# Expert ranks of the first batch moved into the last slot and tail of the first attention of a four-stage kernel

## The chip, the cores and the metric

One core of a Trainium2 chip runs the whole program. The metric is the device time of one execution in microseconds (us); lower is better. Before the change three runs gave 1869.03 (median), 1868.91 and 1872.07 us.

The engines are named as the profile names them: PE (TensorE; PEld is its weight loads), DVE (VectorE), ACT (ScalarE), POOL (GpSimd) and SP (the queue that issues the transfers).

## What is computed

Four residual stages run over 4 batches of 256 tokens of width 512, all in float32. Cut to what matters:

```python
x = x + attention0(layernorm(x))   # 32 query heads, 8 key heads, causal softmax
x = x + experts(layernorm(x))      # 64 experts of rank 16, top 16 of each token
x = x + attention1(layernorm(x))   # RMS norms of q and k, slopes on the distance
x = x + ffn(layernorm(x))          # 4-bit codes times block maxima, silu(g) * u

def experts(x):
    scores = x @ Wr.T
    gates = softmax(top_k(scores, 16))
    h = einsum('nd,krd->nkr', x, A)          # the "ranks"
    return einsum('nkr,kdr->nd', h * G[:, :, None], B) * SCALING
```

## The kernel before

Each float32 product is made of three PE instructions on a high and a low half of each operand (`mm3`, lines 312 to 314). So every operand is first split: a copy to `..._hi` on ACT or POOL, and a subtraction to `..._lo` on DVE or POOL.

Each attention runs over 8 groups of 4 heads, with one key head to a group. Inside a group there is one **slot** for each batch. A slot computes masked scores and softmax of its batch, multiplies the slot before's probabilities with the values (`pv`), adds the slot before's output to `x` (`out` 0 and 1), and makes three weight tiles (K, Q0, Q1 or Q2, Q3, V) of the coming group. The order inside a slot is a hand-written list of steps, one list for all engines: every engine walks the same list and takes from it what is its own (`slot_steps`, `first_slot_steps`, `last_slot_steps`, `tail_steps`, `lead_steps`). An engine does its instructions strictly in that order, and waits on counters (semaphores) of the others. Seven turns of a loop make the slots 1, 2, 3 and 0; a first slot stands ahead, and the last slots 1, 2, 3 and a tail behind it.

Results of PE go through two banks of a ring (`pe_ring_bank`): a tile may start once the tile two places before was read by DVE. So the tile Q1 waits for `kt_lo`, the low half of the tile K.

The first attention also decodes a part of the last stage's weights beside its own work: in each slot POOL centres the codes (`code_early`, line 537), ACT makes eight lines of them in two halves of four (`dq_lines` 0 and 1, line 546), DVE takes their maxima (`dq_top`), and POOL multiplies (`dq_value`). In the second attention POOL splits the next weights (`w_next`, lines 570 and 571) and the normed keys (`k_norm` on POOL, line 1019 and then 570 and 571), for whose end the next slot's scores wait (line 705).

Between two stages the layer norm of each batch runs: `norm_stats` on DVE, `norm_root` on POOL (some 16 short steps, one after the other), `norm_write` on ACT (`xn`, line 473), and `norm_turn`, in which PE transposes `xn` (line 460) and ACT and DVE split the result into `xt_hi` and `xt_lo` (lines 483 and 490). In the last slots batch 0 is normed in slot 2, batch 1 in slot 3, batch 2 in the tail, and batch 3 in the next stage.

The experts' stage (`expert_steps`) splits the router's matrix and the matrix A in pieces (`split_a` 0 to 4: ACT to `a_hi`, DVE to `a_lo`, lines 1328 and 1402), POOL writes the pattern `spread`, then PE makes the router's scores and the ranks of each batch in 4 units of 24 matmuls. DVE's `router` makes the gates from the scores, ACT and DVE split them (`turn_gates`), and PE spreads them (`gated`, lines 1300 and 1302). The two transfers of A and the router's matrix are issued by SP at 653 us of the trace, during the last slot 1.

Semaphores keep memory apart: `a_hi`, `a_lo` and `ranks` lie where the first attention's queries and keys lay.

## Time and profile before

| what | us |
|---|---|
| median of three runs | 1869.03 |
| lowest and highest run | 1868.91, 1872.07 |
| the profiled execution, its own time | 1863.55 |
| its span in the trace | 1861.8 |
| PE busy | 1751.9 (94%) |
| DVE busy | 1296.9 (70%) |
| ACT busy | 877.7 (47%) |
| POOL busy | 788.6 (42%) |

The trace is of one execution. Its span leaves out 1.75 us around it. Busy time of PE counts matmuls, whose ends are modelled. A wait in the trace is idle time of an engine ahead of one instruction, put down to the instruction that ended it.

### The profile page before, as it was taken

To read this page: it belongs to the slowest core of one execution; us is meant where nothing else is said; L and a number is where in the kernel's file an instruction comes from. 1 tells how busy PE (TensorE), PEld (TensorE's weight loads), DVE (VectorE), ACT (ScalarE), POOL (GpSimd) and SP (SyncE) were. 2 spreads that over 40 slices of the span, in tenths; PEclk is the share of its full clock that TensorE was granted. 3 is DMA by queue.
4 is the path that set the end of the run, shared out by engine and by line. 5 is a ranking of instruction groups with operands and counts; after the bars stand their busy time and mean duration, and the time that the engine had idled before them with its cause. 6 is when DMAs were issued, how large, how long until landed. Compare 5 with 4: busy or idle time off the path is not lost.

```text
span 1861.8 us, 28756 instructions
## 1 busy us (share of the span) xinstructions
PE 1751.9 (94%) x8864; PEld 1449.6 (78%) x8864; DVE 1296.9 (70%) x2317; ACT 877.7 (47%) x2288; POOL 788.6 (42%) x924
## 2 busy tenths in 40 slices
PE   8999999999999977997899999999999997889999
PEld 7787878788787866885778787878787886668887
DVE  5787778777788765345677777877777776655555
ACT  3556565556555634222444444444444444454543
POOL 5334425262534433144545454545454424244442
PEclk9999999999999998999899999999999999999999
DMA  4022122121112121000101000000001002022121
GB/s 143 33 68 73 60 64 90 43 95 65 62 62 77 47 71 57 1 7 23 35 29 28 28 29 28 28 28 28 28 28 28 23 0 80 0 69 68 56 56 46
DMA packets 47711, 87.77 MB, mean 47 GB/s; under 512 B 6576, under 2 KB 6576, under 8 KB 47536
## 3 DMA queue, kind: packets, MB, share of 16 engines
q1 hardware_dynamic: 47664, 87.19, 14.8%
q8 instruction: 24, 0.39, 0.1%
q14 instruction: 23, 0.19, 0.0%
HBM read 77.73 MB, written 9.44 MB: 47 GB/s over the span
## 4 chain that ended last, share of the span: by engine, by line
PE 54%; DVE 6%; POOL 4%; ACT 3%; issue 2%; POOLq 0%; DVEq 0%; ACTq 0%
PE ring L312 10%; PE ring L314 9%; PE ring L313 9%; PE scores L312 3%; PE scores L314 3%; PE scores L313 3%; PE turned L312 3%; PE turned L313 3%; PE turned L314 3%; PE scores L705 2%; PE turned L791 1%; PE turned L755 1%; PE turned L756 1%; PE turned L777 1%; PE turned L784 1%
## 5 line engine op out<-in xcount | busy, mean ns | idle before, releaser
L312 PE MATMUL ring<-xt_hi,w_lo 128*128 128x512 f32 x768 | 306.3, 399 | 18.9 <-DVE kt_lo L930 14.9
L313 PE MATMUL ring<-xt_lo,w_hi 128*128 128x512 f32 x768 | 304.7, 397 | 0.0
L314 PE MATMUL ring<-xt_hi,w_hi 128*128 128x512 f32 x768 | 304.5, 397 | 0.0
L312 PE MATMUL ring<-wd_hi,ot_lo 128*128 128x512 f32 x512 | 208.3, 407 | 8.2 <-DVE ot_lo L906 6.4
L804 ACT CAST pt_hi<-turned 128x512 fp32r<-128x512 f32 x192 | 100.6, 590 | 237.7 <-PE turned L784 231.0
L313 PE MATMUL ring<-wd_lo,ot_hi 128*128 128x512 f32 x512 | 203.7, 398 | 0.0
L314 PE MATMUL ring<-wd_hi,ot_hi 128*128 128x512 f32 x512 | 203.6, 398 | 0.0
L312 PEld LDWEIGHTS ring<-xt_hi,w_lo 128*128 128x128 f32 x768 | 145.6, 190 | 53.9 <-issue 19.1
L570 POOL TENSOR_SCALAR sq_hi<-sq 128x512 fp32r<-128x512 f32 x80 | 55.0, 687 | 305.4 <-ACT sq L830 286.9
L314 PEld LDWEIGHTS ring<-xt_hi,w_hi 128*128 128x128 f32 x768 | 145.3, 189 | 34.9
L546 ACT ACTIVATE lv_early<-code_early 128x512 f32<-128x512 f32 x224 | 122.6, 631 | 102.9 <-POOL code_early L537 95.0
L313 PEld LDWEIGHTS ring<-xt_lo,w_hi 128*128 128x128 f32 x768 | 145.7, 190 | 31.4
L900 DVE TENSOR_TENSOR p<-p,rsum 128x512 f32<-128x512 f32 (+1 forms) x128 | 150.1, 1173 | 4.4
L862 DVE TENSOR_TENSOR pt_lo<-turned,pt_hi 128x512 fp32r<-128x512 f32 x192 | 120.8, 683 | 35.9 <-ACT pt_hi L804 35.9
L830 ACT ACTIVATE sq<-ring 128x512 f32<-128x512 f32 x80 | 48.3, 604 | 191.6 <-PE ring L314 183.5
L813 ACT ACTIVATE p<-scores,bias,root 128x128 f32<-128x128 f32 (+1 forms) x256 | 128.0, 519 | 19.0 <-DVE bias L890 19.0
L561 POOL TENSOR_TENSOR deq_early<-lv_early 128x512 f32<-128x512 f32 x28 | 37.9, 1354 | 228.8 <-DVE lv_early L555 196.9
L571 POOL TENSOR_TENSOR w_lo<-w_raw,w_hi 128x512 fp32r<-128x512 f32 x96 | 130.2, 1356 | 8.0
L930 DVE TENSOR_TENSOR qt_lo<-ring,qt_hi 128x512 fp32r<-128x512 f32 x128 | 88.1, 688 | 61.7 <-ACT qt_hi L840 60.3
L911 DVE TENSOR_TENSOR x<-x,ring 128x512 f32<-128x512 f32 x128 | 87.0, 682 | 53.4 <-PE ring L314 52.8
L570 POOL TENSOR_SCALAR w_hi<-w_raw 128x512 fp32r<-128x512 f32 x96 | 77.0, 802 | 110.9 <-DMA w_raw<-w_attn_dram 57.4
L906 DVE TENSOR_TENSOR ot_lo<-turned,ot_hi 128x512 fp32r<-128x512 f32 x128 | 83.5, 685 | 57.7 <-ACT ot_hi L819 57.6
(247 smaller groups left out, 4480.6 us busy)
## 6 DMA issues: line engine op xcount, KB each, us to landing
w_raw<-w_attn_dram SPq DMA_DIRECT2D x96, 256.0 KB, 3.1
wd_raw<-w_dense_dram SPq DMA_DIRECT2D x64, 256.0 KB, 2.7
code_early<-codes_dram SPq DMA_DIRECT2D x28, 256.0 KB, 2.8
absmax_early<-absmax_dram SPq DMA_DIRECT2D x56, 128.0 KB, 3.0
kept_dram<-deq_early SPq DMA_DIRECT2D x28, 256.0 KB, 2.0
stage<-kept_dram SPq DMA_DIRECT2D x28, 256.0 KB, 2.7
code_late<-codes_dram SPq DMA_DIRECT2D x14, 256.0 KB, 2.7
absmax_late<-absmax_dram SPq DMA_DIRECT2D x28, 128.0 KB, 2.9
```

What stands on the lines that cost most here:

```text
L312: nc.tensor.matmul(o, l_lo, r_hi, start=start, stop=False)
L313: nc.tensor.matmul(o, l_hi, r_lo, start=False, stop=False)
L314: return nc.tensor.matmul(o, l_hi, r_hi, start=False, stop=stop)
L546: ins = nc.scalar.activation(lv[:, q, :], code[:, par, :], ACT.Copy, bias=offset, scale=scale)
L570: pool_link(nc.gpsimd.tensor_scalar(dst_hi, src, 1.0, 0.0, ALU.mult, ALU.add))
L571: nc.gpsimd.tensor_tensor(dst_lo, src, as_f32(dst_hi), ALU.subtract).then_inc(sem_done, 1)
L804: nc.scalar.copy(pt_hi[:, j, :, :], turned[:, j, :, :]).then_inc(s_pt_hi, 1)
L813: ins = nc.scalar.activation(pr[:, h, :], sc[:, h, :], ACT.Exp, bias=bias[:, k, h:h + 1], scale=scale, accum_out=sums[:, k, h:h + 1])
L862: nc.vector.tensor_tensor(pt_lo[:, j, :, :], turned[:, j, :, :], as_f32(pt_hi[:, j, :, :]), ALU.subtract).then_inc(s_pt_lo, 1)
L900: nc.vector.tensor_tensor(pr[:, :, :], pr[:, :, :], rsum[:, k, :].unsqueeze(2).to_broadcast([P, HEADS, width]), ALU.mult).then_inc(s_prob, 1)
L911: dve_ring_free(nc.vector.tensor_tensor(x[:, t, :], x[:, t, :], tile, ALU.add))
L930: dve_ring_free(nc.vector.tensor_tensor(lo, tile, as_f32(hi), ALU.subtract))
```

## The change

It rewrites the lists of steps; of computing instructions none is added or taken away. The parts:

1. **Slot 2 of the first attention**: the first half of the code lines (`dq_lines` 0) stands behind `pv` on ACT, as in slot 1 already, and no longer ahead of the tile K.
2. **First slots**: in the first attention the second softmax part (`exp` 1) and its normalising stand ahead of the tiles Q0 and Q1; in the second one `normalise` 1 stands ahead of `q_rms` and `v_turn`.
3. **Slot 3 of the second attention**: POOL splits the normed keys ahead of the two next weight tiles.
4. **Last slots of both**: `norm_write` of a batch stands one slot later, behind the probabilities' split, and `norm_turn` behind `pv`. In slot 1 of the second, `k_norm` stands behind the code splits and `out` 1.
5. **First attention into the experts**: `split_a` 0 to 2 in the last slot 3, `split_a` 3 and 4, `spread` and the first two units of batch 0's ranks in the tail. They now wait for the last scores of the attention rather than for its last ring tile. `norm_turn` 2 and the other two units stand in the experts' stage, ahead of and behind the router's step, and `norm_turn` 3 behind the first `gated`.
6. **Second attention into the last stage**: `norm_turn` 2 stands behind the first `unit` (24 matmuls).
7. `b_hi` and `b_lo` lie behind the experts' small buffers.

```diff
-    s = [("pt_split",)] + ([] if rms or b == 1 else [("dq_lines", 0)])
+    s = [("pt_split",)] + ([] if rms or b in (1, 2) else [("dq_lines", 0)])
...
-    s += [("pv",)] + ([("exp", 1)] if rms else [("dq_lines", 0)] if b == 1 else [])
+    s += [("pv",)] + ([("exp", 1)] if rms else [("dq_lines", 0)] if b in (1, 2) else [])
...
+    s += [("k_norm", 1 if b == 1 else 0)] if roots else []
     s += [("w_next", X) for X in (Q0, Q1)] if rms and b == 3 else []
-    s += [("k_norm", 1 if b == 1 else 0)] if roots else []
...
-        s += [("w_next", Q0)] + softmax[2] + [("tile", V, 1, 0), ("q_rms", 1, 1), ("w_next", Q1), ("v_turn", 1)]
-        return s + [("normalise", 1)] + [("w_next", X) for X in (Q2, Q3, V)] + [("transpose",)]
-    s = softmax[0] + [("tile", K, 1, 0)] + softmax[1] + [("tile", Q0, 1, 0)] + softmax[2] + [("tile", Q1, 1, 0)]
-    return s + [("normalise", 1), ("dq_first",), ("transpose",)]
+        s += [("w_next", Q0)] + softmax[2] + [("tile", V, 1, 0), ("normalise", 1), ("q_rms", 1, 1), ("w_next", Q1)]
+        return s + [("v_turn", 1)] + [("w_next", X) for X in (Q2, Q3, V)] + [("transpose",)]
+    s = softmax[0] + softmax[1][0:1] + [("tile", K, 1, 0)] + softmax[1][1:] + softmax[2] + [("tile", Q0, 1, 0)]
+    return s + [("normalise", 1), ("tile", Q1, 1, 0), ("dq_first",), ("transpose",)]
...
-    s = [("pt_split",)] + ([("norm_turn", 0)] if b == 3 else []) + ([("scores", 0)] if b == 1 else [])
+    s = [("pt_split",)] + ([("norm_write", 0, "act")] if b == 3 else []) + ([("scores", 0)] if b == 1 else [])
...
-        s += [("mask", 0), ("pv",)]
+        s += [("mask", 0), ("pv",)] + ([("norm_turn", 0)] if b == 3 else [])
...
-    s += [("normalise", 0), ("exp", 1), ("normalise", 1), ("out", 0)]
-    s += [("k_norm", 1)] if rms and b == 1 else []
+    splits = [("expert", ("split_a", p)) for p in range(3)] if b == 3 and not rms else []
+    s += [("normalise", 0), ("exp", 1), ("normalise", 1)] + splits[0:2] + [("out", 0)] + splits[2:3]
...
-    s += [("norm_write", b - 2, "act")] if b >= 2 else []
-    s += [("out", 1)] + ([("scores", 1)] if b < 3 else [])
+    s += [("out", 1)] + ([("k_norm", 1)] if rms and b == 1 else []) + ([("scores", 1)] if b < 3 else [])
...
-def tail_steps():
-
-    return [("pt_split",), ("norm_turn", 1), ("pv",)] + norm_begin([2], "pool") + [("norm_write", 2, "act"), ("out", 0), ("out", 1),
-                                                                 ("norm_turn", 2)]
+def tail_steps(rms):
+
+    if rms:
+        s = [("pt_split",), ("norm_write", 1, "act"), ("pv",), ("norm_turn", 1)] + norm_begin([2], "pool")
+        return s + [("out", 0), ("out", 1), ("norm_write", 2, "act")]
+    s = [("pt_split",), ("expert", ("split_a", 3)), ("norm_write", 1, "act"), ("expert", ("spread",))]
+    s += [("expert", ("ranks", 0, 0)), ("pv",), ("norm_turn", 1), ("expert", ("split_a", 4))]
+    s += norm_begin([2], "pool") + [("expert", ("ranks", 0, 1)), ("out", 0), ("out", 1), ("norm_write", 2, "act")]
+    return s
...
-            s = [("split_a", 0)] + head(0) + [("split_a", p) for p in range(1, UNITS + 1)] + [("router", 0)]
-            s += norm_begin([3], "pool") + ranks(0)[0:2] + [("norm_write", 3, "act")] + ranks(0)[2:4]
-            s += [("norm_turn", 3)]
-            s += gated(0) + [("router", 1)] + [("split_b", p) for p in range(UNITS)] + ranks(1) + [("out", 0)]
+            s = [("scores", 0)] + ranks(0)[2:3] + [("turn_scores", 0), ("norm_turn", 2), ("router", 0)]
+            s += norm_begin([3], "pool") + ranks(0)[3:4] + [("norm_write", 3, "act")]
+            s += gated(0) + [("norm_turn", 3), ("router", 1)] + [("split_b", p) for p in range(UNITS)] + ranks(1) + [("out", 0)]
...
-                            eng.wait_ge(s_ring_free, attention_tiles[0])
+                            eng.wait_ge(s_scores, GROUPS * BATCH)
...
-            opening += norm_begin([3], "dve") + [("silu", 0), ("h", 0), ("h_hi", 0), ("norm_turn", 3), ("h_lo", 0)]
+            opening += [("norm_stats", [3]), ("norm_root", [3], "dve"), ("norm_turn", 2), ("norm_write", 3, "dve")]
+            opening += [("silu", 0), ("h", 0), ("h_hi", 0), ("norm_turn", 3), ("h_lo", 0)]
```

How the built instructions move, at three places. **ACT, slot 2 of the first attention's loop.** `lv_early` are the code lines, `kt`, `qt` the tiles K and Q0 (then Q1), `p` the softmax, `ot` the product `pv`. Before:

```order
L804 CAST pt_hi<-turned 128x512
L543 REGISTER_ALU
L546 ACTIVATE lv_early<-code_early 128x512 x4
L368 REGISTER_ALU
L835 COPY kt_f<-ring 128x256
L836 CAST kt_hi<-ring 128x512
```

With the change:

```order
L813 CAST pt_hi<-turned 128x512
L372 REGISTER_ALU
L844 COPY kt_f<-ring 128x256
L845 CAST kt_hi<-ring 128x512
...
L822 ACTIVATE p,sums<-scores,bias 128x256 x4
L828 CAST ot_hi<-turned 128x512 x2
L550 ACTIVATE lv_early<-code_early 128x512 x4
L372 REGISTER_ALU
L848 COPY qt_f<-ring 128x256
L849 CAST qt_hi<-ring 128x512
```

The four lines moved from ahead of the tile K to ahead of the copies of the tile Q1.

**ACT, from the first attention's tail to the experts' first gates.** Before:

```order
L819 CAST ot_hi<-turned 128x512 x2
L473 ACTIVATE xn<-x,shift,rstd 128x512 x2
L483 CAST xt_hi<-ring 128x4x128 x2
L1328 CAST a_hi<-a_raw 128x4x64
L1328 CAST a_hi<-a_raw 128x4x256 x4
L1336 ACTIVATE gate<-score,top_neg 128x64 x2
L1346 COPY ranks<-scores 128x512 x2
L473 ACTIVATE xn<-x,shift,rstd 128x512 x2
L1346 COPY ranks<-scores 128x512 x2
L483 CAST xt_hi<-ring 128x4x128 x2
L1352 CAST gates_hi<-scores 64x256
```

With the change:

```order
L1339 CAST a_hi<-a_raw 128x4x256
L1357 COPY ranks<-scores 128x512
L477 ACTIVATE xn<-x,shift,rstd 128x512 x2
L1357 COPY ranks<-scores 128x512
L487 CAST xt_hi<-ring 128x4x128 x2
L1347 ACTIVATE gate<-score,top_neg 128x64 x2
L1357 COPY ranks<-scores 128x512
L477 ACTIVATE xn<-x,shift,rstd 128x512 x2
L1363 CAST gates_hi<-scores 64x256
```

The splits of A and two of the four copies of ranks went ahead; the last `xn` here is batch 3's, and `gates_hi` still stands right behind it, with one unit of ranks ahead of it in place of four.

**POOL, slot 3 of the second attention's loop.** Before:

```order
L570 TENSOR_SCALAR w_hi<-w_raw 128x512
L340 REGISTER_ALU
L571 TENSOR_TENSOR w_lo<-w_raw,w_hi 128x512
L1017 REGISTER_ALU
L1019 TENSOR_SCALAR kt_f<-k_raw 128x256
L570 TENSOR_SCALAR kt_hi<-k_raw 128x512
```

With the change:

```order
L1032 TENSOR_SCALAR kt_f<-k_raw 128x256
L574 TENSOR_SCALAR kt_hi<-k_raw 128x512
L344 REGISTER_ALU
L575 TENSOR_TENSOR kt_lo<-k_raw,kt_hi 128x512
L574 TENSOR_SCALAR w_hi<-w_raw 128x512
```

The keys' three instructions moved ahead of the four of the next weights Q0 and Q1.

## Rows read from the trace of the kernel before

**Rows 1.** The profile's page, its first part: busy us, share, instructions.
```profile
PE 1751.9 (94%) x8864; PEld 1449.6 (78%) x8864; DVE 1296.9 (70%) x2317; ACT 877.7 (47%) x2288; POOL 788.6 (42%) x924
```

**Rows 2.** Busy PE, PEld, DVE, ACT, POOL, then clock: first attention's end.
```profile
660.00:741.00 81.00, 61.69 (x331) 51.41 (x330) 46.65 (x96) 33.20 (x77) 23.86 (x109) 0.85 0.11 42
```

**Rows 3.** PE's waits over the whole trace: total us, times, longest.
```profile
PE ring L312 <- DVE kt_lo L930: 14.9, 6, 2.7
PE ring L460 <- ACT xn L473: 14.9, 7, 3.5
PE scores L705 <- POOL kt_lo L571: 10.7, 7, 1.7
...
PE turned L777 <- DVE q_slope L960: 4.1, 1, 4.1
```

**Rows 4.** Timeline, PE, starts of slots 2 and 3, first and second loop turn.
```profile
75.44 0.39 PE L705 MATMUL scores<-kt_f,qt_f 128*128 128x128 f32 x2
...
95.16 0.39 PE L705 MATMUL scores<-kt_f,qt_f 128*128 128x128 f32 x2
...
155.03 0.39 PE L705 MATMUL scores<-kt_f,qt_f 128*128 128x128 f32 x2
...
179.17 0.39 PE L705 MATMUL scores<-kt_f,qt_f 128*128 128x128 f32 x2
```

**Rows 5.** Timeline, ACT and PE in slot 2 of the second turn.
```profile
163.90 0.63 ACT L546 ACTIVATE lv_early<-code_early 128x512 f32<-128x512 f32 x1 [7.97 <-POOL code_early L537]
...
167.68 0.49 PE L312 MATMUL ring<-xt_hi,w_lo 128*128 128x512 f32 x1 [2.52 <-DVE kt_lo L930]
```

**Rows 6.** Timeline, PE, starts of slots 3 and 0, second attention, first and seventh turn.
```profile
950.94 0.28 PE L705 MATMUL scores<-kt_f,qt_f 128*128 128x128 f32 x1
...
975.56 0.38 PE L705 MATMUL scores<-kt_f,qt_f 128*128 128x128 f32 x1 [1.70 <-POOL kt_lo L571]
...
1493.77 0.39 PE L705 MATMUL scores<-kt_f,qt_f 128*128 128x128 f32 x2
...
1516.50 0.28 PE L705 MATMUL scores<-kt_f,qt_f 128*128 128x128 f32 x1
```

**Rows 7.** Timeline, PE, the waits ahead of the second transposes of both first slots.
```profile
51.56 1.97 PE L791 MATMUL turned<-ident,p 128*128 128x128 f32 x8 [2.86 <-DVE p L900]
...
904.69 1.97 PE L791 MATMUL turned<-ident,p 128*128 128x128 f32 x8 [2.49 <-DVE p L900]
```

**Rows 8.** PE's waits from 660 to 741 us, the first three.
```profile
PE ring L460 <- ACT xn L473: 9.0, 4, 3.5
PE turned L312 <- DVE pt_lo L862: 4.5, 3, 1.7
PE ring L312 <- DVE xt_lo L490: 3.6, 2, 2.3
```

**Rows 9.** Busy time by stretch, the stretches at half clock between 660 and 741.
```profile
679.00:686.00 7.00, 5.78 (x14) 4.59 (x15) 5.17 (x9) 2.37 (x5) 0.00 (x0) 0.52 0.00 0
696.00:702.00 6.00, 4.77 (x15) 3.82 (x16) 3.60 (x6) 3.73 (x8) 0.00 (x0) 0.50 0.00 0
713.00:723.00 10.00, 6.70 (x30) 6.14 (x31) 6.59 (x9) 4.58 (x6) 4.83 (x7) 0.50 0.00 1
```

**Rows 10.** Groups by line and shape, 700 to 760 us: busy us, mean ns.
```profile
L1402 DVE TENSOR_TENSOR a_lo<-a_raw,a_hi 128x1024 fp32r<-128x1024 f32 x4 | 4.6, 1218 | 0.0
```

**Rows 11.** Timeline, DVE and ACT, batch 3's norm and the first gates.
```profile
726.56 1.28 DVE L399 BATCH_NORM_STATS2 bn<-x 128x6 f32<-128x512 f32 x2
...
732.59 1.52 ACT L473 ACTIVATE xn<-x,shift,rstd 128x512 f32<-128x512 f32 x2 [4.81 <-POOL shift L448]
...
735.91 0.38 ACT L1352 CAST gates_hi<-scores 64x256 fp32r<-64x256 f32 x1
...
736.79 0.40 DVE L1410 TENSOR_TENSOR gates_lo<-scores,gates_hi 64x256 fp32r<-64x256 f32 x1
```

**Rows 12.** PE's waits from 1540 to 1620 us, the first.
```profile
PE ring L460 <- ACT xn L473: 5.9, 3, 2.7
```

More of the change, by code:

```diff
@@ L1175, in expert_steps @@
         def expert_steps():
-            head = lambda b: [("scores", b), ("turn_scores", b)]
             ranks = lambda b: [("ranks", b, u) for u in range(UNITS)]
@@ L1243, in sp, with pe_steps @@
                 eng.dma_start(b_raw, lora_b).then_inc(s_lora_raw[1], 16)
-            def pe(eng):
-                scores_at = 0
-                for step in expert_steps():
-                    b = step[1]
+            scores_at, out_at = [0], [0]
+            def pe_steps(eng, steps):
+                for step in steps:
+                    b = step[1] if len(step) > 1 else None
                     if step[0] == "scores":
@@ L1317, in pe, with act_steps @@
                         pe_norm_turn(eng, b)
-            def act(eng):
-                out_at = 0
-                for step in expert_steps():
-                    b = step[1]
+            def act_steps(eng, steps):
+                for step in steps:
+                    b = step[1] if len(step) > 1 else None
                     if step[0] in ("split_a", "split_b"):
@@ L1365, in act, with pool_steps @@
                         act_ring.take()
[L1366 removed]
+                        out_at[0] = act_ring.n
                     elif step[0] in NORM_STEPS:
                         act_norm(eng, step)
[L1370 to L1381 removed]
+            def pool_steps(eng, steps):
+                for step in steps:
+                    if step[0] == "spread":
+                        eng.wait_ge(s_scores, GROUPS * BATCH)
+                        ones = ranks[0:EXPERTS, EC // 2:EC, :].rearrange("p c d -> p (c d)")
+                        pool_link(nc.gpsimd.memset(ones, 1.0))
+                        pool_link(nc.gpsimd.affine_select(out=ones, in_=ones, compare_op=ALU.is_ge, fill=0.0, base=0,
+                                                          pattern=[[1, ER]], channel_multiplier=-RANK))
+                        pool_link(nc.gpsimd.affine_select(out=ones, in_=ones, compare_op=ALU.is_ge, fill=0.0,
+                                                          base=RANK - 1, pattern=[[-1, ER]], channel_multiplier=RANK))
+                        nc.gpsimd.tensor_scalar(spread[:, :], ones, 1.0, 0.0, ALU.mult, ALU.add).then_inc(s_spread, 1)
+                    elif step[0] == "gated":
                         eng.wait_ge(s_gated_hi, UNITS * step[1] + step[2] + 1)
@@ L1394, in pool, with dve_steps @@
                         pool_norm(eng, step)
-            def dve(eng):
-                for step in expert_steps():
-                    b = step[1]
+            def dve_steps(eng, steps):
+                for step in steps:
+                    b = step[1] if len(step) > 1 else None
                     if step[0] in ("split_a", "split_b"):
@@ L1454, in router, with pe, act, dve @@
                                         ALU.mult).then_inc(s_gates, 1)
+            behind_first["pe"], behind_first["act"] = pe_steps, act_steps
+            behind_first["dve"], behind_first["pool"] = dve_steps, pool_steps
+            def pe(eng):
+                pe_steps(eng, expert_steps())
+            def act(eng):
+                act_steps(eng, expert_steps())
+            def dve(eng):
+                dve_steps(eng, expert_steps())
+            def pool(eng):
+                pool_steps(eng, expert_steps())
             return pe, act, dve, pool, sp
```

41 lines of the change are left out of this document (19 added, 22 removed).

## The prediction, made before the changed kernel ran

> **What bounds the kernel now.** I read the page's first part first: PE is busy for 1751.9 of 1861.8 us [rows 1]. So PE is the bound, and what a change of order can win is the 110 us in which PE stands, and stretches in which its clock is halved. The other engines have room on the whole (DVE 70%), so the question is only where they are late for PE. PE's waits over the whole trace answer that [rows 3]: `kt_lo` on DVE 14.9 us in 6 waits, `xn` on ACT 14.9 in 7, `kt_lo` on POOL 10.7 in 7. The first and the third repeat 6 or 7 times, which says "loop", the second belongs to the ends of the attentions. The end of the first attention is the worst place: PE is busy for 61.7 of 81 us at a mean clock of 0.85 [rows 2]. The change touches all of these places. I go through it by place.
>
> **Loop of the first attention, slot 2 (part 1).** The starts of the scores give the length of a slot. Slot 2 takes 95.16 − 75.44 = 19.72 in the first turn, and 179.17 − 155.03 = 24.14 in the second [rows 4]; the later ones are alike (their mean is 24.10). Slots 1, 3 and 0, which have the same matmuls, also take about 20. What is lost is seen on ACT [rows 5]: it sits idle for 7.97 until POOL has centred the codes (`code_early`), then makes four lines (0.63 the first, 2.2 together), and only then copies the tile K. So `kt_lo` comes late, and PE waits 2.52 ahead of Q1's matmuls; six such waits make the 14.9 [rows 3]. The rest of the 4.4 is a wait for `ot_lo` or PE at half clock behind the wait. With the change ACT goes to the tile K at once. The gain is at most 6 × (24.10 − 19.72) = 26.3.
>
> Some is given back. The four lines, 2.2, now stand behind `pv` and ahead of the copies of tile Q1. So `qt_hi` comes up to 2.2 later, with it `qt_lo` and the next normalising on DVE, and the maxima that POOL's next centring waits for. By my count PE feels 0.8 of it in each slot 2, in all 7 turns: 5.6. Slot 1 has this very order and takes 20, which excludes more than about 2 in a slot while the centre is on time. Term: −26.3 + 5.6 = **−20.7**; bounds −26.3 (nothing given back) and −11 (the whole 2.2 in each turn).
>
> **Loop of the second attention, slot 3 (part 3).** The slot takes 975.56 − 950.94 = 24.62 in the first turn, and 1516.50 − 1493.77 = 22.73 in the seventh [rows 6]. In the seventh there are no next weights to split, so POOL's queue is free: that measures the slot without the queue. The first ends in a wait of 1.70 for POOL's `kt_lo`, one of seven [rows 3]. With the keys ahead of four POOL instructions the wait is gone, and the weights are needed a slot later, so nobody waits for them instead. Term: 6 × (24.62 − 22.73) = **−11.4**; bounds −11.4 and −8 (the six waits of 1.70 less some loss elsewhere).
>
> **First slots (part 2).** PE waits 2.86 and 2.49 for the normalised `p` [rows 7]. In the second attention the normalising jumps two items of DVE and the wait goes whole; in the first only an exponential and one tile's subtraction are passed, of which I expect 1.6. Term: −1.6 − 2.5 = **−4.1**; bounds −5.3 and −1.5.
>
> **From the first attention's last slots to the experts (parts 4, 5).** This is one stretch, from the last transposes of slot 2 to the first ranks of batch 1. PE's work in it at full clock stays. Its three largest sorts of wait are `xn` 9.0, `pt_lo` 4.5, `xt_lo` 3.6: together 17.1 [rows 8]. And the clock is at 0.50 in three stretches, in which PE is busy for 5.78 + 4.77 + 6.70 us; half of that, 8.6, is lost [rows 9]. With the change `xn` is written a slot ahead of its transposes and ranks stand in the gaps, so these waits go. New ones come:
>
> - the tail's `pv` waits for `pt_lo`, behind which DVE now has pieces of A, at 1.218 each [rows 10]: 1.5;
> - in slot 3 two short ones, for `pt_lo` 1.7 and for the ring's `xt_lo` 0.9, and two of 0.75 together;
> - the first gates' transposes wait for DVE's router, since only two units of ranks are left to stand over it: 1.9;
> - the first `gated` waits for `gates_lo`. Before, 736.79 + 0.40 − 726.56 = 10.6 us passed from the start of batch 3's statistics to the end of `gates_lo`; without the copies in between it is 6.0 to the start of `xn`, 2 × 0.76 for `xn`, 0.38 and 0.40 for the two halves of the gates: 8.4 [rows 11]. Four units of ranks lay over it; now PE has only 1.9 us of work there (the gates' transposes and batch 1's scores). Wait: 8.4 − 1.9 = 6.5.
>
> New waits: 1.5 + 3.35 + 1.9 + 6.5 = 13.3, so waits win 17.1 − 13.3 = 3.8. Clock: the stretches at half clock lie behind pauses of PE. The first two have no such pause any more; behind the one of 6.5 I expect one like the last, 6.70 / 2 = 3.4. That wins 8.6 − 3.4 = 5.2. Term: **−9.0**; bounds −14 (the gates are met in time, no half clock) and −3 (half clock stays as it is and the short waits double).
>
> The rule of the Trainium skill, "TensorE: Matmul & The Clock Gate", section "What's actually happening", speaks against this: "the default state is throttled, and activity releases the throttle", so a new gap charges more than its length. The trace agrees as far as it goes, with 0.50 behind the present gaps.
>
> **End of the second attention (parts 4, 6).** The three waits for `xn`, 5.9 us [rows 12], go in the same way, and so do those that follow from them; some 0.6 comes for `pt_lo`: −5.3. Against it stands the last slot 1: its `k_norm` now follows two code splits on POOL and `out` 1, while the next scores wait for the keys. Before, PE waited 4.1 there for `q_slope` [rows 3]; I expect 5.5, so +1.4. Term **−3.9**; bounds −6 and +1.
>
> Part 7 moves memory alone; SP's queue has the same transfers in the same order, and A is loaded at 653, ahead of its first new split. I cost both at nothing.
>
> **Sum.** −20.7 − 11.4 − 4.1 − 9.0 − 3.9 = −49.1. The profiled execution took 1863.55, so 1814.5; the median of the runs lies 5.5 above that execution, so 1820.0. All bounds low: 26.3 + 11.4 + 5.3 + 14 + 6 = 63.0, 1806. All high: 11 + 8 + 1.5 + 3 − 1 = 22.5, 1846.5.
>
> **Rivals.**
>
> *A, the lines pile up.* ACT now has both halves of the code lines behind `pv`, close together. If the chain of centring, lines and maxima then runs late in each turn, the gain of slot 2 comes back as later waits for `ot_lo` and `p`: 26.3 − 7 × 2.7 leaves 7 us in place of 20.7, 1834. For it speaks that the lines waited for POOL by 7.97 [rows 5]; against it slot 1.
>
> *B, the boundary gives nothing.* The gap of 6.5 at the first gates plus PE at half clock for as long as in the last stretch, and one more such stretch at the tail: the term is between 0 and −4, and the time 1825 to 1829. For it speaks that the gates' half is still queued behind batch 3's `xn` on ACT.
>
> *C, slower.* The decoding of the early weights is one chain per tile (POOL centres, ACT makes two halves, DVE takes two maxima, POOL multiplies). By my count a tile takes 20.1 us, as long as a slot, and the wait at slot 2 was its slack. If moving the lines back makes this chain the bound, each of the 28 slots is longer. It decides from (26.3 + 28.3) / 28 = 1.95 us a slot, the 28.3 being the other terms (11.4 + 4.1 + 9.0 + 3.9, rounded); at 2.5 a slot the result is 70 − 54.7 = +15.3, 1884. Against it: slots 1, 3 and 0 take the same 20 us with the chain running beside them.
>
> *D, nothing is given back.* The copies of Q1 have slack: 1814.
>
> **How the numbers follow.** Forecast 0.60, A 0.15, B 0.15, D 0.07, C 0.03. The range reaches over D's neighbourhood and A: 1808 to 1837, leaving out C and the outer ends of the bounds. A measurement of this kernel tells 0.2%, 3.7 us, from no change. All cases but C are faster by far more; of their 0.97 I keep 0.01 for a mixture that comes out even: 0.96, 0.01 and, for C, 0.03.
>
> **What the changed profile would show.** Right: slot 2 of the first attention takes some 20.5 in all seven turns and `kt_lo` on DVE is gone from PE's waits; slot 3 of the second takes 22.7 in all; batch 1's ranks start near 732; one wait of 6 to 7 for `gates_lo` ahead of the first `gated`. A shows as waits of 2 to 3 for `ot_lo` or `p` in slots 2 and 3; B as a clock of 0.5 from 720 on; C as slots of 22 us throughout. If slot 2 still takes 24, or if the lines are found to wait for POOL again and hold back `qt_hi`, the largest term is wrong.

## The result, and the profile after

The changed kernel takes 1813.65 us (median of 4 runs, 1807.24 to 1818.03); the kernel before, run beside it, 1868.97. The ratio is 0.9699, with a 95% interval from 0.9666 to 0.9732: 3.0% faster. Predicted were 1820.0 and a range of 1808 to 1837. The profiled execution took 1811.87 (span 1810.2), where the sum made for it said 1814.5.

The page's first part, beside [rows 1]:

```profile
PE 1736.5 (96%) x8864; PEld 1443.1 (80%) x8864; DVE 1295.3 (72%) x2317; ACT 877.6 (48%) x2288; POOL 787.8 (44%) x924
```

PE has the same instructions and is busy 15.4 us less, so a part of the gain is clock. The granted clock is given as a share of full speed: 1.00 is full, 0.50 half, and a value between them is the mean of a stretch that has both. Over the whole trace it rose from 0.981 to 0.986. An estimate from these two means: (1 − 0.981) × 1861.8 = 35.4 us of full speed were withheld before and (1 − 0.986) × 1810.2 = 25.3 now, 10 less, a part of it in PE's pauses. PE's waits over the whole trace (total us, times, longest), beside [rows 3]:

```profile
PE turned L316 <- DVE pt_lo L873: 9.8, 6, 1.9
PE scores L712 <- POOL kt_lo L575: 6.4, 1, 6.4
PE turned L1312 <- DVE gates_lo L1421: 6.3, 1, 6.3
```

The three waits that led the list are gone: `kt_lo` on DVE with its 14.9, `xn` on ACT with its 14.9, and the seven for POOL's `kt_lo` (what stands there now is one other wait, in the second attention's last slot 1). Timeline of PE, the starts of slots 2, 3 and 0 in the second turn of the first attention, beside [rows 4]:

```profile
150.94 0.61 PE L712 MATMUL scores<-kt_f,qt_f 128*128 128x128 f32 x4
...
170.59 0.61 PE L712 MATMUL scores<-kt_f,qt_f 128*128 128x128 f32 x4
...
191.21 0.50 PE L712 MATMUL scores<-kt_f,qt_f 128*128 128x128 f32 x3
```

Slot 2 takes 19.65 in place of 24.14, and slot 3 20.62 in place of 20.11. That holds in all seven turns. Timeline of ACT in that slot 2, beside [rows 5]:

```profile
156.26 0.37 ACT L844 COPY kt_f<-ring 128x256 f32<-128x256 f32 x1 [4.43 <-PE ring L318]
...
162.56 2.25 ACT L550 ACTIVATE lv_early<-code_early 128x512 f32<-128x512 f32 x4
164.65 0.42 ACT L848 COPY qt_f<-ring 128x256 f32<-128x256 f32 x1
```

ACT takes the tile K as soon as PE has made it; the code lines start without any idle time before them. Timeline of PE, start and end of slot 3 in the second attention's first turn, beside [rows 6], and the wait in the first attention's first slot, beside [rows 7]:

```profile
49.85 1.09 PE L798 MATMUL turned<-ident,p 128*128 128x128 f32 x8 [0.97 <-DVE p L911]
...
914.62 0.61 PE L712 MATMUL scores<-kt_f,qt_f 128*128 128x128 f32 x4
...
937.42 0.72 PE L712 MATMUL scores<-kt_f,qt_f 128*128 128x128 f32 x5
```

Slot 3: 22.80, as the seventh turn took before. In the first slot the wait fell from 2.86 to 0.97, and the eight transposes behind it from 1.97 to 1.09: they had run at half clock.

The first gates, timelines of DVE, ACT and PE, beside [rows 11]:

```profile
687.87 1.28 DVE L403 BATCH_NORM_STATS2 bn<-x 128x6 f32<-128x512 f32 x2
...
693.92 1.52 ACT L477 ACTIVATE xn<-x,shift,rstd 128x512 f32<-128x512 f32 x2 [7.74 <-POOL shift L452]
695.35 0.35 ACT L1363 CAST gates_hi<-scores 64x256 fp32r<-64x256 f32 x1
...
696.29 0.55 PE L1312 MATMUL turned<-gates_lo,spread 64*128 64x256 f32 x1 [6.26 <-DVE gates_lo L1421]
```

The gates are whole at 687.95, but their copy waits on ACT until 695.35 behind batch 3's norm. PE waits 6.26, forecast 6.5.

Stretches measured between starts of slots, in us. The kernel before and the changed one, from their profiled executions:

| stretch | before | changed | difference | forecast |
|---|---|---|---|---|
| first attention, first slots | 38.06 | 33.33 | −4.7 | −1.6 |
| first attention, loop | 563.34 | 540.34 | −23.0 | −20.7 |
| its last slots, tail, experts, next opening | 247.69 | 241.78 | −5.9 | −9.0 |
| second attention, first slots | 43.31 | 40.46 | −2.9 | −2.5 |
| second attention, loop | 607.87 | 596.08 | −11.8 | −11.4 |
| its last slots to the end | 324.15 | 320.65 | −3.5 | −3.9 |

With 0.2 lost ahead of the first slot this is the −51.6 of the spans. The forecast of the third row was made for its first part alone, up to the first ranks of batch 1. Each number of the table is of one execution; the experiments show which rows would be different with another.

### The profile page after: what moved, and what is told of

It is laid out like the page before. It is cut to its first block, busy times and chain, and to the rows that moved or that the text cites. A ratio compares the mean times of both kernels' runs of the same rounds, so it can differ in the third digit from the quotient of the medians.

```text
span 1810.2 us, 28744 instructions
## 1 busy us (share of the span) xinstructions
PE 1736.5 (96%) x8864; PEld 1443.1 (80%) x8864; DVE 1295.3 (72%) x2317; ACT 877.6 (48%) x2288; POOL 787.8 (44%) x924
## 4 chain that ended last, share of the span: by engine, by line
PE 56%; DVE 5%; ACT 3%; POOL 2%; issue 1%; DMA 0%; POOLq 0%; DVEq 0%; ACTq 0%; SPq 0%
PE ring L316 10%; PE ring L318 10%; PE ring L317 10%; PE scores L316 3%; PE scores L318 3%; PE scores L317 3%; PE turned L316 3%; PE turned L318 3%; PE turned L317 3%; PE scores L712 2%; PE turned L798 2%; PE turned L791 1%; PE turned L762 1%; PE turned L763 1%; PE turned L784 1%
## 5 line engine op out<-in xcount | busy, mean ns | idle before, releaser
L813 ACT CAST pt_hi<-turned 128x512 fp32r<-128x512 f32 x192 | 100.7, 592 | 234.1 <-PE turned L791 232.4
L316 PEld LDWEIGHTS ring<-wd_hi,ot_lo 128*128 128x128 f32 x512 | 96.4, 188 | 34.8 <-issue 9.3
L899 DVE TENSOR_REDUCE negmax<-scores 128x4 f32<-128x512 f32 (+1 forms) x128 | 121.9, 953 | 2.1
```

Of the source, the lines that this page charges most:

```text
L316: nc.tensor.matmul(o, l_lo, r_hi, start=start, stop=False)
L813: nc.scalar.copy(pt_hi[:, j, :, :], turned[:, j, :, :]).then_inc(s_pt_hi, 1)
L899: dve_link(nc.vector.tensor_reduce(negmax[:, k, :], sc[:, :, :], AX.X, ALU.max, negate=True))
```

## The experiments

All times are medians; the kernel before was run beside each. It gave 1868.55 in the first job (e1 to e4), 1868.52 in the second (e5 to e8), 1864.88 in the third (e9 to e11, another chip) and 1870.05 in the fourth (e12).

### e1_slot2: part 1 alone

```diff
-    s = [("pt_split",)] + ([] if rms or b == 1 else [("dq_lines", 0)])
+    s = [("pt_split",)] + ([] if rms or b in (1, 2) else [("dq_lines", 0)])
-    s += [("pv",)] + ([("exp", 1)] if rms else [("dq_lines", 0)] if b == 1 else [])
+    s += [("pv",)] + ([("exp", 1)] if rms else [("dq_lines", 0)] if b in (1, 2) else [])
```

> The kernel before with part 1 alone: in slot 2 of the first attention ACT makes the first half of the code lines behind pv. Theory (ACT, held up by POOL's centre, delays the tile K's copies, in six of seven turns): slot 2 goes from 24.1 to 19.7 in those six turns, slot 3 from 20.1 to 20.6 in all seven, so 6 x 4.4 - 7 x 0.5 = 23 us less, 1846; everything outside the loop stays. Rival (the first slots' pause or clock sets whether the loop falls into the slow pattern): slot 2 still takes 24 in some turns, and the gain is under 15.

Measured: 1845.52, ratio 0.9872 (0.9854 to 0.9889). In the trace slot 2 takes 19.65 to 19.68 and slot 3 20.58 to 20.64 in every turn, and the loop 540.3. The order on ACT alone explains the loop's gain; the rival falls. That "everything outside the loop stays" did not hold, though its order is that of before. The first attention's first slots take 35.22 in place of 38.06, the second's 44.74 in place of 43.31. In the former PE has the same wait ahead of the second transposes, and another clock behind it. Timeline and busy time by stretch of before, then of e1:

```profile
51.56 1.97 PE L791 MATMUL turned<-ident,p 128*128 128x128 f32 x8 [2.86 <-DVE p L900]
51.00:58.00 7.00, 6.44 (x30) 6.39 (x31) 2.66 (x5) 1.17 (x2) 0.98 (x1) 0.52 0.14 40
...
51.97 1.09 PE L791 MATMUL turned<-ident,p 128*128 128x128 f32 x8 [2.86 <-DVE p L900]
51.40:58.40 7.00, 6.43 (x42) 5.84 (x43) 5.32 (x9) 1.25 (x3) 1.00 (x1) 1.00 0.11 40
```

### e2_keys: part 3 alone

```diff
+    s += [("k_norm", 1 if b == 1 else 0)] if roots else []
     s += [("w_next", X) for X in (Q0, Q1)] if rms and b == 3 else []
-    s += [("k_norm", 1 if b == 1 else 0)] if roots else []
```

> The kernel before with part 3 alone: the keys ahead of the two next weights on POOL in slot 3 of the second attention. Theory (POOL's queue): slot 3 goes from 24.6 to 22.8 in six turns, 11 to 12 us less, 1857.5. Rival (the gain came from the second first slot, or is given back in slot 1, which the changed kernel shows at 23.4 to 23.6): under 8 us.

Measured: 1857.01, ratio 0.9933 (0.9916 to 0.995). Slot 3 takes 22.72 to 22.77 in all seven turns, the loop 596.26. Slot 1 keeps its 23.4, from 23.2 to 23.6 with and without the change, so nothing is given back there.

### e3_loops: parts 1, 2 and 3

Both diffs above and those of the first slots (the change's part 2).

> The kernel before with parts 1, 2 and 3, the ends of both attentions left alone. If the parts add up as they stand in the traces: 23.0 + 11.8 in the loops, 4.7 + 2.9 in the first slots, 42 us less in all, 1827; the ends then owe the remaining 13. Rival (the ends owe less, and the rest is where half-clock stretches happen to fall): 1818 to 1822.

Measured: 1827.01, ratio 0.9769 (0.9751 to 0.9787). The parts add, and what the changed kernel has beyond them (parts 4 to 7, the ends of the attentions) owes the rest, 13 to 15 us of the medians. Part 7 was never run by itself.

### e11_first: part 2 alone

```diff
-        s += [("w_next", Q0)] + softmax[2] + [("tile", V, 1, 0), ("q_rms", 1, 1), ("w_next", Q1), ("v_turn", 1)]
-        return s + [("normalise", 1)] + [("w_next", X) for X in (Q2, Q3, V)] + [("transpose",)]
-    s = softmax[0] + [("tile", K, 1, 0)] + softmax[1] + [("tile", Q0, 1, 0)] + softmax[2] + [("tile", Q1, 1, 0)]
-    return s + [("normalise", 1), ("dq_first",), ("transpose",)]
+        s += [("w_next", Q0)] + softmax[2] + [("tile", V, 1, 0), ("normalise", 1), ("q_rms", 1, 1), ("w_next", Q1)]
+        return s + [("v_turn", 1)] + [("w_next", X) for X in (Q2, Q3, V)] + [("transpose",)]
+    s = softmax[0] + softmax[1][0:1] + [("tile", K, 1, 0)] + softmax[1][1:] + softmax[2] + [("tile", Q0, 1, 0)]
+    return s + [("normalise", 1), ("tile", Q1, 1, 0), ("dq_first",), ("transpose",)]
```

> The kernel before with part 2 alone, both first slots. Theory (the wait for the normalised p, 2.9 and 2.5, and the stretch at half clock behind each): 4.7 in the first attention's first slots, 2.9 to 4.2 in the second's, 7 to 9 us less, 1860.5. By the prediction's term, waits alone, it would be 4.1 less, 1864.5. Rival (slot 2 of the first attention's first turns change too): over 10.

Measured: 1861.06 (10 runs), ratio 0.9973 (0.9958 to 0.9988), which is 5.0 us less, with bounds of 2.2 and 7.8. The timing can't tell the forecast's 4.1 from 7. The trace can: the first attention's first slots take 33.32 and the second's 40.96, so 4.7 + 2.4 are won there against the profiled execution of before, at the expected places. Against e1 (35.22 and 44.74) and e2 (36.62 and 44.68), which have the first slots of before, it is 1.9 + 3.8 and 3.3 + 3.7. It lost some of it in stretches at half clock: 250.8 passed between the attentions, with the order of before, in place of 247.7.

### e4_same: the changed kernel again

> The changed kernel itself, profiled once more. Theory (how long PE stays at half clock behind one and the same pause differs from one execution to the next): same waits within 0.3 us, but stretches at half clock in other places or of other length in the experts' stage and the opening of the second attention, where the first profile showed 5 us more than the kernel before with the same waits; the runs spread by 5 to 10 us again. Rival (the longer stretches come from the order of the work): the same stretches, 760 to 771 and 804 to 825 us, at half clock again.

Measured: 1812.36 (1808.82 to 1815.60), ratio 0.969 (0.9667 to 0.9713). Busy time by stretch, columns as in [rows 9], of the first profile and then of this one:

```profile
696.20:708.70 12.50, 12.32 (x74) 11.64 (x74) 8.63 (x28) 7.38 (x12) 5.01 (x4) 0.72 0.00 1
760.00:771.00 11.00, 11.00 (x80) 10.85 (x79) 7.33 (x26) 3.56 (x7) 7.11 (x15) 0.84 0.01 2
804.00:815.00 11.00, 10.44 (x38) 8.22 (x38) 6.88 (x18) 1.95 (x4) 5.56 (x6) 0.84 0.12 44
```

```profile
696.60:709.10 12.50, 12.44 (x65) 11.97 (x66) 8.63 (x28) 7.42 (x12) 4.99 (x4) 0.60 0.00 1
760.40:771.40 11.00, 11.00 (x80) 10.85 (x79) 7.33 (x26) 3.56 (x7) 7.11 (x15) 0.84 0.01 2
804.40:815.40 11.00, 10.44 (x38) 8.21 (x38) 6.88 (x18) 1.95 (x4) 5.76 (x6) 0.84 0.14 47
```

My theory was half wrong. In the later two windows a stretch at half clock comes back in the same place and of the same length; behind the long pause the length differs (0.72 and 0.60). The second attention's first slots differ too, 41.27 in place of 40.46, where PE waits 2.36 for `xn` ahead of `v_turn` in place of 1.49. So part of it is repeatable, part is not.

The same test for the kernel before came for free, since e1, e2 and e3 keep its order between the attentions. Busy time by stretch over the ranks of batch 1, of before, then of e2, where they start within 0.2 us of the same time:

```profile
734.50:748.50 14.00, 11.71 (x91) 10.54 (x90) 11.18 (x30) 9.61 (x17) 5.04 (x4) 1.00 0.01 1
```

```profile
734.30:748.30 14.00, 12.87 (x59) 11.67 (x58) 8.67 (x29) 7.11 (x13) 5.01 (x4) 0.51 0.00 1
```

Same instructions, same time: 1.00 in the one, 0.51 in the other. But what stood ahead of them differs. In before a stretch at half clock came earlier (0.87 from 720 to 733), and PE waited only 0.72 for batch 3's `xn`; e2 ran that stretch at 1.00, came earlier and waited longer:

```profile
733.55 1.34 PE L460 MATMUL ring<-ident,xn 128*128 128x128 f32 x8 [0.72 <-ACT xn L473]
...
733.21 1.33 PE L460 MATMUL ring<-ident,xn 128*128 128x128 f32 x8 [2.36 <-ACT xn L473]
```

A pair with the same waits ahead is before and e11, later in the experts' stage. In both PE's longest wait in the 12 us ahead is 0.34, and up to there e11 runs within 0.3 us of before for 160 us. Busy time by stretch of before, then of e11:

```profile
786.00:798.60 12.60, 11.83 (x67) 9.40 (x65) 5.39 (x9) 2.67 (x5) 0.73 (x1) 1.00 0.00 0
798.60:801.60 3.00, 3.00 (x26) 2.99 (x26) 2.85 (x16) 1.83 (x4) 3.00 (x3) 1.00 0.01 3
...
782.40:795.00 12.60, 11.84 (x68) 9.51 (x66) 5.28 (x9) 2.68 (x5) 0.64 (x1) 1.00 0.00 0
795.00:798.00 3.00, 3.00 (x15) 2.88 (x14) 2.84 (x16) 1.83 (x4) 3.00 (x3) 0.52 0.01 3
```

From the first attention's last slot 1 to the second one's first scores e1, e2, e3 and e8 take 252.9, 252.7, 253.2 and 252.8; the profiled execution of before took 247.69. It was a lucky one by 5 us, in two places: some 4 us over the ranks of batch 1 and 1.2 behind 858 us. Against these four the changed kernel's 241.8 and 243.4, and the 244.4 of e6 below, which has its order here, are 8.3 to 11.4 less, not 5.9.

### e8_end1: parts 1, 2, 3 and the second attention's share of parts 4 and 6

```diff
-    s = [("pt_split",)] + ([("norm_turn", 0)] if b == 3 else []) + ([("scores", 0)] if b == 1 else [])
+    first = [("norm_write", 0, "act")] if rms else [("norm_turn", 0)]
+    s = [("pt_split",)] + (first if b == 3 else []) + ([("scores", 0)] if b == 1 else [])
...
-        s += [("mask", 0), ("pv",)]
+        s += [("mask", 0), ("pv",)] + ([("norm_turn", 0)] if b == 3 and rms else [])
...
-    s += [("k_norm", 1)] if rms and b == 1 else []
...
-    s += [("norm_write", b - 2, "act")] if b >= 2 else []
+    s += [("norm_write", b - 2, "act")] if b >= 2 and not rms else []
-    s += [("out", 1)] + ([("scores", 1)] if b < 3 else [])
+    s += [("out", 1)] + ([("k_norm", 1)] if rms and b == 1 else []) + ([("scores", 1)] if b < 3 else [])
```

The second attention's tail and the last stage's opening are those of the change.

> The kernel before with parts 1, 2, 3 and the second attention's share of parts 4 and 6; the first attention's end stays as it was. Theory: 3.5 us less than with parts 1 to 3 alone (the stretch from the second attention's last slot 1 to the end took 324.5 there and 320.6 to 321.4 in the changed kernel): 1823.5; so parts 4 and 5 at the first attention's end are worth the remaining 11, of which 5 come from a stretch of ranks at half clock that the first trace of the kernel before did not have. Rival (the ends of the second attention win nothing, the first one's all): 1827.

Measured: 1824.37, ratio 0.9759 (0.9731 to 0.9788). The median is 2.6 lower than with parts 1 to 3, within what the timing can tell; the stretch to the end is 320.6 in place of 324.5. By difference, and not by a run of their own, parts 4, 5 and 7 at the first attention's end owe the other 11 to 12.

### e5_gates: the first gates ahead of batch 3's norm

```diff
-            s += norm_begin([3], "pool") + ranks(0)[3:4] + [("norm_write", 3, "act")]
-            s += gated(0) + [("norm_turn", 3), ("router", 1)] + [("split_b", p) for p in range(UNITS)] + ranks(1) + [("out", 0)]
+            s += ranks(0)[3:4] + gated(0)[0:2] + norm_begin([3], "pool") + [("norm_write", 3, "act")]
+            s += gated(0)[2:] + [("router", 1)] + [("split_b", p) for p in range(UNITS)] + ranks(1)[0:2]
+            s += [("norm_turn", 3)] + ranks(1)[2:4] + [("out", 0)]
```

> The changed kernel with the first gates put ahead: their two halves stand ahead of batch 3's norm on ACT and DVE, and batch 3's transposes behind two units of batch 1's ranks. Theory (the pause of 6.3 us ahead of the first gated is batch 3's norm standing ahead of the gates on ACT, and PE runs at half clock behind it, at a price of 3.8 to 5.5): the pause falls under 1.5, the half clock behind it goes, 8 to 10 us less than the changed kernel, 1804. Rival (the pause is held by the router on DVE): under 2 us. Second rival (the half clock comes anyway, behind the wait of 2.4 for the gates): 5 us less.

Measured: 1804.63 (1803.51 to 1806.58), ratio 0.9659 (0.9638 to 0.9681). Timeline of ACT:

```profile
688.47 0.37 ACT L1364 CAST gates_hi<-scores 64x256 fp32r<-64x256 f32 x1 [2.27 <-PE scores L1301]
697.02 1.52 ACT L477 ACTIVATE xn<-x,shift,rstd 128x512 f32<-128x512 f32 x2 [8.19 <-POOL shift L452]
```

`gates_hi` is made 6.9 us earlier, the wait for `gates_lo` is gone, and from last slot 1 to the next first scores 234.3 us pass in place of 241.8 and 243.4. The pause was the order on ACT, as the forecast had it. The half clock did not go: busy time by stretch, same columns,

```profile
688.00:702.90 14.90, 14.43 (x82) 13.61 (x83) 8.68 (x29) 6.25 (x12) 6.88 (x19) 0.66 0.01 2
```

shows 0.66 behind the remaining wait of 2.4 for the gates. So the first theory has the wait right and the clock wrong, and the second rival the clock right: it comes anyway. Its 5 us were too few, since 7.5 to 10 were won at the place.

### e9_filled and e12_filled24: the pause filled with idle matmuls

```diff
                         if n == 0:
                             eng.wait_ge(s_spread, 1)
+                            for k in range(48):
+                                nc.tensor.matmul(gate_banks[0][:, 0, 0:P], ident[:, :], ident[:, :], start=True, stop=True)
```

with 48 in the first and 24 in the second.

> The changed kernel with 48 matmuls of the identity with itself on PE in the pause ahead of the first gated; their result is written over. They remove no wait for the gates and no work, they only keep PE busy for some 5.7 of the 6.3 us. Theory (the pause costs its length and, on top, PE at half clock behind it): gated starts at the same time, batch 1's ranks run at full clock, 4 us less, 1808 to 1809. Rival (what stands behind the pause is slow for a reason of its own, or the half clock comes later instead): 0 to 1 us, the same time as the changed kernel.

Measured: 1816.68, ratio 0.9742 (0.9726 to 0.9758), slower than the changed kernel. The fill was too long: each matmul made two passes, 10.9 us together. The gates were met 4.2 us late. So its time answers nothing on the cost of the half clock, though its trace shows 1.00 behind the fill, from 701.4 to 711.2 us.

> The changed kernel with 24 matmuls of the identity in the pause ahead of the first gated, in place of 48. In the run with 48 each took two passes of the array, 10.9 us together, so that PE came 4.6 us late to the gates; 24 take 5.4 and fit into the pause of 6.3. Theory (half clock behind the pause is the pause's doing): gated starts at the same time as in the changed kernel, and from there to the end of the first two units of batch 1's ranks 9.7 us pass, as with 48, in place of 12.3; 2.6 us less, some 0.15% of the time, which the timing can hardly tell, the trace can. Rival (the half clock stays or only moves behind the next wait): 12.3 again, or 9.7 and then a half-clock stretch behind the wait for the copies of the ranks.

Measured: 1812.69, ratio 0.969 (0.9665 to 0.9716), no difference from the changed kernel that the timing tells. Busy time by stretch in e12, from the first `gated` to the end of the second two units of ranks, and the wait between (timeline of PE), then the same of the changed kernel:

```profile
696.70:706.50 9.80, 9.51 (x76) 8.81 (x74) 7.12 (x24) 5.82 (x10) 5.04 (x4) 1.00 0.01 2
706.50:716.30 9.80, 7.27 (x50) 7.26 (x50) 5.01 (x7) 3.55 (x6) 0.00 (x0) 0.83 0.01 2
...
709.04 0.58 PE L316 MATMUL scores<-xt_hi,a_lo 128*128 128x256 f32 x1 [2.53 <-ACT ranks L1359]
```

```profile
696.20:706.50 10.30, 10.21 (x58) 9.74 (x59) 6.56 (x23) 5.18 (x10) 5.01 (x4) 0.67 0.01 2
706.50:715.70 9.20, 8.03 (x67) 7.83 (x67) 5.67 (x9) 4.29 (x6) 0.00 (x0) 1.00 0.00 0
```

With the pause filled, here and in e9, PE runs at full clock behind it, so the half clock there is indeed the pause's doing. And it buys nothing: the first half is 2.6 us shorter, PE then waits 2.53 for ACT's copies of the ranks in place of 1.17, and half clock behind that wait takes some 1.2 us more. So a half of the gain goes to ACT and a half to the clock again, as the rival had it. From the start of `gated` to the end of the ranks it is 19.50 us with the fill and 19.43 without.

### e6_lastkeys: the keys of the last slot 1 earlier

```diff
-    s += [("normalise", 0), ("exp", 1), ("normalise", 1)] + splits[0:2] + [("out", 0)] + splits[2:3]
+    if rms and b == 1:
+        s += [("normalise", 0), ("exp", 1), ("out", 0), ("k_norm", 1), ("normalise", 1)]
+    else:
+        s += [("normalise", 0), ("exp", 1), ("normalise", 1)] + splits[0:2] + [("out", 0)] + splits[2:3]
...
-    s += [("out", 1)] + ([("k_norm", 1)] if rms and b == 1 else []) + ([("scores", 1)] if b < 3 else [])
+    s += [("out", 1)] + ([("scores", 1)] if b < 3 else [])
```

> The changed kernel with the keys of the second attention's last slot 1 normed ahead of the second normalising, of out 1 and of the code splits on POOL. Theory (the wait of 6.4 for the keys is POOL's two code splits, the normalising of 1024 columns, slowed by them, and two additions ahead of the keys): the wait falls to about 3.5 or moves to q_slope, 3 us less, and if the half clock behind it goes too, 5 us less: 1808 to 1811. Rival (the wait just moves to the next step, the normalised p ahead of the transposes): 0 to 1 us.

Measured: 1812.13 (1808.20 to 1812.87), ratio 0.969 (0.9667 to 0.9714), no difference that the timing tells. The trace has 318.3 to the end in place of 320.7: 2.4 won. The wait of 6.4 became one of 3.9 for `q_slope`, and the half clock behind it went. PE's timeline and the slot behind the wait, of the changed kernel, then that slot of e6:

```profile
1511.04 2.05 PE L712 MATMUL scores<-kt_f,qt_f 128*128 128x128 f32 x8 [6.38 <-POOL kt_lo L575]
1511.04:1527.77 16.73, 13.90 (x66) 11.89 (x66) 10.36 (x25) 7.15 (x22) 1.21 (x5) 0.87 0.00 1
...
1513.41:1528.03 14.62, 11.81 (x67) 9.78 (x67) 11.02 (x26) 7.13 (x22) 3.43 (x7) 1.00 0.13 37
```

So the slot with the wait is 0.9 shorter (21.49 to 20.57) and the next one 2.1, of which some is given back near the end, where PE waits 4.53 for `w_lo` in place of 3.00. What held up the keys then, from the timelines of DVE and POOL in e6:

```profile
1509.71 1.23 DVE L914 TENSOR_TENSOR p<-p,rsum 128x1024 f32<-128x1024 f32 x1
...
1509.75 1.45 POOL L1035 TENSOR_SCALAR kt_f<-k_raw 128x256 f32<-128x256 f32 x1 [10.05 <-DVE k_raw L981]
```

and in the changed kernel:

```profile
1504.45 2.16 DVE L911 TENSOR_TENSOR p<-p,rsum 128x1024 f32<-128x1024 f32 x1
...
1504.26 3.47 POOL L1517 TENSOR_TENSOR w_lo<-stage,w_hi 128x512 fp32r<-128x512 f32 x2 [7.64 <-ACT w_hi L1511]
...
1508.56 0.41 POOL L1032 TENSOR_SCALAR kt_f<-k_raw 128x256 f32<-128x256 f32 x1 [0.82 <-DVE k_raw L978]
```

The same copy to `kt_f` takes 0.41 with DVE's `p` out of the way and 1.45 when it starts 0.04 us behind it; `p` takes 1.23 ahead of POOL and 2.16 beside it. The Trainium skill, "SBUF — State Buffer", section "Who interferes with whom", says that a DVE instruction with two inputs from SBUF contends with a GpSimd instruction that reads it, and that it is an exclusive lock. The traces agree. In e6 `p` started first and kept its 1.23, and POOL's copy took 1.0 longer. In the changed kernel POOL started first, `p` took 0.9 longer, and POOL's pair took 3.47 for two instructions whose like (`kt_lo`) takes 1.26. That this contention sets the time of PE's wait is not shown.

### e7_both and e10_best

e7 has the edits of e5 and e6. e10 adds the scores of batch 1 ahead of the first gates' transposes:

```diff
+                s = [("scores", b + 1), ("turn_gates", b)] if b == 0 else [("turn_gates", b), ("scores", b + 1)]
-                return [("turn_gates", b), ("scores", b + 1)] + units[0:1] + [("turn_scores", b + 1)] + units[1:]
+                return s + units[0:1] + [("turn_scores", b + 1)] + units[1:]
```

> Both of these edits on the changed kernel. The two places are 800 us apart, so the gains should add: 11 to 14 us less than the changed kernel, 1800. If half clock falls in other places instead: some 8 less.

> Both edits of the earlier run (first gates ahead of batch 3's norm, keys of the last slot 1 ahead) and the scores of batch 1 ahead of the transposes of the first gates on PE. Theory: the wait of 2.4 for the gates falls to about 0.9, as 1.5 us of scores lie over it, and the gates' halves are no longer covered by them (0.4): 1 us less than both edits alone; with less half clock behind it 2: 1803. Rival (half clock stays): same as both edits, 1804.6.

Measured: e7 1804.61 (1800.34 to 1807.12), ratio 0.9651 (0.9625 to 0.9677); e10 1799.76 (1797.84 to 1806.55), ratio 0.9658 (0.964 to 0.9677). PE's waits between the attentions in e10:

```profile
PE scores L319 <- ACT ranks L1362: 1.1, 1, 1.1
PE scores L1305 <- DVE gate L1468: 1.0, 1, 1.0
...
PE turned L1317 <- DVE gates_lo L1426: 1.0, 1, 1.0
```

The wait for the gates fell from 2.4 to 1.0, and 1.0 for `gates_lo` came; the stretch is 234.1 us, as in e5. In e7 the stretch is 237.6, as half clock comes in two later places (near 758 and 801 us). By their ratios e5, e7 and e10 can't be told apart, so the gains of the two edits did not show as a sum, and 1800 for e7 was a miss. All three lie below the changed kernel, by 6 to 9 us at their ratios of 0.965 to 0.966 against 0.969 to 0.970, though the intervals touch. The traces show 7.5 to 10 us at the place of the edit in e5 and e10, and 4 to 7 in e7. e10's lower median stands beside a kernel before that was lower too.

## Why the prediction was right, and where it was off

**Slot 2 of the first attention** (forecast −20.7): −23.0. The mechanism and the full gain of 26 came as forecast. What is given back I put at 0.8 in each of seven slots; it was 0.51 (20.62 − 20.11), 3.6 in all. It shows in slot 3 and nowhere else, where I had looked for it in slot 2 (20.5 forecast, 19.65 measured); why it comes there was not tested. Rival A, a pile of lines with 2.7 a turn, did not happen, and C, the decoding chain as the bound, neither: slots 1 and 0 keep their 20.1 and 19.7.

**Slot 3 of the second attention** (−11.4): −11.8. Measuring it by the seventh turn, where the cause was absent, was worth more than adding up waits (10.7).

**First slots** (−4.1): −7.6 against the profiled execution of before, outside the bounds given. The step that failed is that no wait was given a clock behind it. Behind the wait of 2.86 PE had run eight transposes in 1.97 in place of 1.09, and then the scores' eight products of 128 columns in 1.92 in place of 1.06 and their 12 of 256 in 2.90 in place of 1.68; this half clock went with the wait. I had counted it for the last slots and forgot it here. The wait itself fell by 1.9 (1.6 forecast). But the size is in part luck of the traces: in e1 the same wait of 2.86 had full clock behind it, in e2 a part of it. Over all pairs of an old and a new order that were profiled the gain is 5.2 to 7.6. The second attention's wait of 2.49 did go whole, as forecast, but PE then waits longer for `xn` ahead of `v_turn`, 1.49 in place of 0.77 (1.97 in e11, 2.36 in e4), which I had at nothing.

**The first attention's end** (−9.0). Up to the first ranks of batch 1 it is −11.0 (65.8 before, 54.8 now). The waits are what was forecast: 6.3 for `gates_lo` (6.5), 2.4 for the gates (1.9), 1.7 and 1.0 for `pt_lo` (1.7 and 1.5), 1.1 and 0.4 for the rest. Of the 17.1 that were to go, the 4.5 for `pt_lo` held one of 1.72 in slot 2, which lies ahead of this stretch and is still there; four small ones (1.9 together) that I had left out make up for it. The sign "batch 1's ranks start near 732" was worked out wrongly: it takes the 9 off the old trace's 741 and not the 27.5 won ahead of it, and they start at 702.3.

The later parts of the same stretch were 5 us longer than in the trace of before. Three stretches at half clock make some 4.3 of it, behind 761, 805 and 823 us. The last one e1, e2, e3 and e8 have too, with the order of before. The first two they do not have, and e11, also with that order, has both; the changed kernel has them in both of its executions. So they are not the change's alone, but whether it makes them more frequent stays open. Against e1, e2, e3 and e8 the end wins 8.3 to 11.4. Rival B, a boundary that gives nothing, is refuted by that. The rule of the Trainium skill that I weighed there ("TensorE: Matmul & The Clock Gate", section "What's actually happening"), that activity releases the throttle, agrees with e9 and e12, where the clock was full behind the filled pause. The trace of e11 goes beyond it, since there the clock fell while PE was busy. What the half clock would cost was decided by the next wait, for ACT's copies of the ranks, and the half clock behind that one.

**The second attention's end** (−3.9): −3.5, which is two errors that cancel. Its cost in last slot 1 was forecast as 1.4 and is 1.5, though the wait is 6.4 and not 5.5. But behind that wait PE is at half clock, and the next slot takes 16.73 in place of 14.69, another 2.0 that I had at nothing. What remains gained 7.0, and not 5.3.

**From the execution to the median.** I added 5.5 to the sum, the distance of the profiled execution of before from its median. The changed kernel's lies 1.8 from its own. This is the larger part of the 6 us by which 1820 was too high: 3.7 from here and 2.6 from the terms. The distance is no constant of the kernel. In the first job's runs of before, time goes with the mean granted clock: 1865.74 at 0.978, 1868.55 at 0.975, 1871.75 at 0.973. It does so only roughly: of e11's runs one took 1857.03 at 0.978 and one 1860.96 at 0.980. The clock explains a large part of an execution's distance from the median, and that distance should have been left as width of the range. The terms of the sum hang on one execution too. Beside e1 and e2 the one of before was 5 us short between the attentions, 1.4 short in the second attention's first slots, and 1.4 to 2.8 long in the first's. That the sum came within 2.6 of the two traces is therefore in part luck.

## What to carry over

Where one turn of a loop lacks the cause of a wait (the first turn of slot 2, the last turn of slot 3), the difference of slot lengths prices the fix better than the waits do, since it holds the half clock and the waits that follow too. For slots that run once, a half clock behind a wait belongs to the range: it came in some executions and not in others. An instruction that makes way for an urgent one must be looked at in its turn: here batch 3's norm went ahead of the gates' copy on ACT, stood there with 6.3 us of pause, and PE had work over only a part of it; with the gates ahead of the norm 7.5 to 10 us were won there (e5). And before a stretch of one profile is compared with one of another, look at its clock in several executions: 5 us of this kernel lie in that alone.

## What the runs showed of the hardware

The same instructions, with the same waits ahead of them, ran at full clock in one execution and at half clock in another: 0.52 in before and 1.00 in e1 behind the wait of 2.86 in the first slots, 1.00 in before and 0.52 in e11 near 799 and 795 us. Some such stretches come back in the same place (760 to 771 us in both executions of the changed kernel), others come and go. How much of the spread of 5 to 11 us between runs they make is not shown, as only one run of a kernel was profiled each time. The Trainium skill says in "TensorE: Matmul & The Clock Gate", section "What's actually happening", that the number of slow matmuls varies from run to run; the traces here agree.

Half clock does not need a pause of PE ahead of it. In e11 it came after 25 us at 1.00 in which PE was busy for 24.24 and never waited longer than 0.34:

```profile
770.00:795.00 25.00, 24.24 (x152) 20.98 (x151) 8.22 (x19) 5.85 (x10) 3.96 (x18) 1.00 0.00 1
```

A pause of PE and the half clock behind it can both be free: with the pause filled PE was 2.6 us faster, and then lost as much to a longer wait for ACT and to half clock behind that (e12).

Matmuls of 128 by 128 float32 with plain operands took 0.23 each, and the trace has two records for each (e9: 96 records in 10.9 us).
